# A decoder layer on one core: smaller ScalarE units, resident output weights, keys summed earlier, and a new order of all queues

## What is computed

```python
x = layernorm(x + mamba_and_mlp(x))      # block 1
x = layernorm(x + cross_attention(x, ctx, ctx))  # block 2
x = layernorm(x + lora_experts(x))       # block 3

# block 1
h = x + mamba(rmsnorm(x, w_n1))
#   u, z = split(xn @ in_proj.T); u = silu(causal_conv4(u) + b)
#   dt_r, B, C = split(u @ x_proj.T); dt = softplus(dt_r @ dt_proj.T + b)
#   state[t] = exp(dt[t] * A) * state[t-1] + dt[t] * B[t] * u[t]   (16 states a channel)
#   y = sum over states of state * C + u * D;  out = (y * silu(z)) @ out_proj.T
return h + (silu(hn @ w1.T) * (hn @ w2.T)) @ w3.T      # hn = rmsnorm(h, w_n2)

# block 2: 16 heads, 64 keys. The temperature of the second softmax is a small MLP of three
# means per head over the whole sequence of 1024 queries: mean score, mean of the row maxima,
# mean variance of the first softmax's probabilities
t = exp(clip(mlp(mean_sim, max_sim, entropy_proxy)))
out = softmax(qk / (2 t)) @ V @ Wo.T

# block 3: 8 experts, top 2 by a gate, rank 16, beside a dense matmul
```

## Time and profile before

| what | value |
|---|---|
| median of 3 runs | 3610.53 us (3606.46 to 3612.91) |
| the profiled execution | 3614.06 us, span 3612.0 us, clock of TensorE 0.921 on average |
| TensorE busy | 3056.7 us (85%) |
| VectorE busy | 2799.0 us (77%) |
| ScalarE busy | 2137.4 us (59%) |
| GpSimd busy | 2535.8 us (70%) |
| DMA | 558.49 MB, 47.4% of 16 engines' time |

### The profile page before, as it was taken

One profiled execution on the slowest core, in us unless ns is written; L12 is line 12 of the kernel. 1 busy time (PEld: TensorE's weight loads), 2 busy tenths in 40 slices (PEclk: granted clock), 3 DMA queues, 4 the chain that ended last, 5 costly groups with the idle time before them and its releaser, 6 DMA issues.

```text
span 3612.0 us, 33154 instructions
## 1 busy us (share of the span) xinstructions
PE 3056.7 (85%) x8248; PEld 1460.9 (40%) x8248; DVE 2799.0 (77%) x3376; ACT 2137.4 (59%) x4824; POOL 2535.8 (70%) x1132
## 2 busy tenths in 40 slices
PE   6877677877988987899989868998994898999868
PEld 3433333333434433444434334444442444444444
DVE  3778888888898888888899888888898898822253
ACT  4666666565558457766774586666547857441132
POOL 0557877779998897778889978787798888810000
PEclk9988888889998999999989979999996999999989
DMA  4455555556654564454655634545453444522100
GB/s 174 145 171 201 188 187 199 186 188 221 221 186 147 174 210 132 129 164 147 195 154 184 204 111 146 166 149 177 160 190 110 162 159 162 168 76 76 41 1 24
DMA packets 247160, 558.49 MB, mean 155 GB/s; under 512 B 34748, under 2 KB 35132, under 8 KB 246716
## 3 DMA queue, kind: packets, MB, share of 16 engines
q1 hardware_dynamic: 246972, 556.38, 47.4%
HBM read 515.91 MB, written 40.37 MB: 154 GB/s over the span
## 4 chain that ended last, share of the span: by engine, by line
PE 38%; DVE 10%; ACT 9%; issue 4%; POOL 2%; DMA 0%; DVEq 0%; ACTq 0%; POOLq 0%; SPq 0%
PE ps L1781 22%; PE ps L1878 8%; DVE hb L1558 3%; PE ps L1839 3%; ACT ps L1428 2%; ACT xw L1467 2%; DVE ps L1568 1%; PE ps L1949 1%; PE ps L1914 1%; ACT ps L1252 1%; POOL hb L1194 1%; DVE mxs L1640 1%; PE ps L1982 1%; POOL hb L1204 1%; PE ps L1941 1%
## 5 line engine op out<-in xcount | busy, mean ns | idle before, releaser
L1204 POOL TENSOR_TENSOR hb<-hb,bc 128x1024 f32<-128x1024 f32 x512 | 1205.5, 2355 | 390.4 <-ACT state L1322 225.3
L1194 POOL TENSOR_TENSOR hb<-dtu,bc 128x1024 f32<-128x1024 f32 x512 | 1206.3, 2356 | 161.1 <-DVE ps L1568 153.2
L1781 PE MATMUL ps<-fT,wden 128*128 128x512 f32 x2304 | 1044.4, 608 | 78.9 <-DVE se L1653 25.7
L1252 ACT ACTIVATE ps<-dt,a_neg 128x512 f32<-128x512 f32 x1024 | 689.2, 690 | 588.0 <-DVE hb L1558 586.5
L1781 PEld LDWEIGHTS ps<-fT,wden 128*128 128x128 f32 x2304 | 442.6, 195 | 632.6 <-issue 611.1
L1558 DVE TENSOR_TENSOR_SCAN hb<-ps,state,hb 128x512 f32<-128x512 f32 x512 | 627.6, 1268 | 73.0 <-POOL hb L1194 38.8
L1558 DVE TENSOR_TENSOR_SCAN hb<-ps,hb 128x512 f32<-128x512 f32 x512 | 596.8, 1207 | 88.4 <-POOL hb L1194 63.8
L1568 DVE TENSOR_TENSOR ps<-ps,hb 128x1024 f32<-128x1024 f32 x512 | 624.6, 1220 | 11.6 <-POOL hb L1204 10.9
L1781 PE MATMUL ps<-xnT,wmix 128*128 128x512 f32 x1024 | 492.7, 642 | 81.6 <-DMA wmix<-in_w_mix 44.1
L1878 PE MATMUL ps<-wden,hm 128*128 128x512 f32 x1024 | 466.2, 608 | 34.2 <-DVE res L1611 14.8
L1781 PEld LDWEIGHTS ps<-xnT,wmix 128*128 128x128 f32 x1024 | 208.5, 207 | 361.9 <-issue 305.4
(11 more groups left out here) (248 smaller groups left out, 3535.1 us busy)
## 6 DMA issues: line engine op xcount, KB each, us to landing
bc<-p_dram SPq DMA_DIRECT2D x1024, 256.0 KB, 3.4
wden<-in_w SPq DMA_DIRECT2D x192, 512.0 KB, 4.0
wmix<-in_w_mix SPq DMA_DIRECT2D x128, 512.0 KB, 3.9
z_dram<-ring SPq DMA_DIRECT2D x64, 256.0 KB, 4.5
u<-z_dram SPq DMA_DIRECT2D x32, 512.0 KB, 5.0
watt<-in_w_qof SPq DMA_DIRECT2D x26, 512.0 KB, 4.5
u_dram<-res SPq DMA_DIRECT2D x24, 512.0 KB, 3.4
u<-u_dram SPq DMA_DIRECT2D x24, 512.0 KB, 5.2
```

The lines of the kernel that those rows point to most:

```text
L1194: TTn(hb[:, n % HB], dtu[:, :, :], bc[:, 0, n % BC].unsqueeze(1).broadcast_to([P, 2, CH]), ALU.mult).then_inc(s.s1_ready, 1)
L1204: TTn(hb[:, n % HB], hb[:, n % HB], bc[:, 1, n % BC].unsqueeze(1).broadcast_to([P, 2, CH]), ALU.mult).then_inc(s.s3_done, 1)
L1252: A_(dst, dt[:, p % 2, jj], ACT.Exp, scale=a_neg[:, j, n:n + 1]).then_inc(full_of(key), 1)
L1781: ins = M(dst, a, b, start=start and n == 0, stop=stop and n == len(pairs) - 1)
```

## The change

Seven edits, in the words of the code:

1. `norm`, `xs` and `hs` become four units each, one for each tile. `out` of a chunk writes its Squares to the lower half of `xnT` for every chunk, and `hs` too.
2. `sp1` is cut in two: `sp0` (Abs, Exp) and `sp1` (the two Identities).
3. The four weight tiles of `ou` are loaded once (`load_o`), when the last `z` is done, to the two slots of `wmix` and the upper half of `xnT`. The 64 loads go.
4. `kmean` sums the keys and multiplies them with the summed queries. It stands in stream `s` behind the scores of the first tile. `mean` keeps the two reductions over maxima and variances.
5. `WORK` and `PHASE` are replaced.
6. `LOOK` is replaced.
7. The costs in `parts` follow the new units.

```diff
-    got = [("norm", c), ("xs", c)] + [("tin", c, n) for n in range(KC)]
+    got = [("norm", c, t) for t in range(TT)] + [("xs", c, t) for t in range(TT)] + [("tin", c, n) for n in range(KC)]
...
-        got += [("rms", c), ("hs", c)] + [("to", c, n) for n in range(KC)]
+        got += [("rms", c)] + [("hs", c, t) for t in range(TT)] + [("to", c, n) for n in range(KC)]
...
-    return [("dt", c, j), ("sp1", c, j), ("sp2", c, j), ("sp3", c, j), ("sp4", c, j)]
+    return [("dt", c, j), ("sp0", c, j), ("sp1", c, j), ("sp2", c, j), ("sp3", c, j), ("sp4", c, j)]
...
+            if t == 0 and c % 2:
+                got.append(("kmean", c))
...
     if kind == "norm":
-        part(ACT_, 5.2, ("x_load", c), ("z", c - 2, JB - 1))
-        part(DVE, 0.2, mine())
+        part(ACT_, 0.85 if i < last else 2.6, ("x_load", c), ("z", c - 2, JB - 1))
+        if i == last:
+            part(DVE, 0.2, mine())
     elif kind == "xs":
-        part(ACT_, 3.2, ("norm", c))
+        part(ACT_, 0.8, ("norm", c, last))
...
-        part(PE, 4 * MM, ("gate", c, PAIRS - 1), ("res_load", c), ("f_load", F_FIRST.get(u)),
+        part(PE, 4 * MM, ("gate", c, PAIRS - 1), ("res_load", c), ("o_load", 0),
...
+    elif kind == "sp0":
+        before_c, before_p = pair_of(c * PAIRS + i // 2 - 1)
+        part(ACT_, 1.3, ("dt", *key), ("sp4", c, i - 1) if i % 2 else ("sp4", before_c, 2 * before_p + 1), ("yp", before_c, before_p))
     elif kind == "sp1":
...
-        part(ACT_, 2.68, ("dt", *key), ("sp4", c, i - 1) if i % 2 else ("sp4", before_c, 2 * before_p + 1), ("yp", before_c, before_p))
+        part(ACT_, 1.45, ("sp0", *key))
...
+    elif kind == "kmean":
+        part(DVE, 2.6, ("kv", b))
     elif kind == "mean":
-        part(DVE, 4.0, ("ent", c))
+        part(DVE, 1.0, ("ent", c))
...
-WORK = {"x": 849.2, "w": 145.7, "s": 1219.5, "y": 59.6, "f": 162.7}
+WORK = {"x": 1925.7, "w": 118.4, "s": 1411.9, "y": 1558.6, "f": 210.1}
...
-    "f": (2.25, 28.227, 8.121, 13.061, 16.33, 4.66, 5.08, 6.078),
...
+    "f": (1.383, 20.274, 10.618, 15.423, -9.517, 4.439, 5.932, 6.466),
...
-        elif kind == "ou":
-            first[u] = len(src)
-            src.append(W_O + u[3])
-            release.append((u, u))
...
-LOOK = {"m": 0.319, "l": 0.0, "x": 0.0, "w": 0.043, "s": 0.009, "y": 0.096, "f": 0.0}
+LOOK = {"m": 0.09, "l": 0.037, "x": 0.018, "w": 0.023, "s": 0.043, "y": 0.047, "f": 0.041}
...
+    at(DONE[("z", CHUNKS - 1, JB - 1)], 1, "o_load", 0)
...
+        w_o = [wmix[:, 0], wmix[:, 1]] + [xnT[:, 1, 2 * m:2 * m + 2].rearrange("p c l -> p (c l)") for m in range(2)]
...
+            def load_o():
+
+                filled(sp, ("z", CHUNKS - 1, JB - 1))
+                for q in range(PAIRS):
+                    sp.dma_start(w_o[q], A["w_mix"][W_O + q]).then_inc(s.wo_in, 16)
...
                     ch.link(A_(sp_e, src, ACT.Abs))
-                    ch.link(A_(sp_e, sp_e, ACT.Exp, scale=-1.0))
+                    A_(sp_e, sp_e, ACT.Exp, scale=-1.0).then_inc(s.e_ready, 1)
+                elif kind == "sp1":
+                    act.wait_ge(s.e_ready, c * JB + i + 1)
...
-                elif kind == "mean":
+                elif kind == "kmean":
                     dve.wait_ge(kv_in[b % 2], 64 * (b // 2 + 1))
-                    dve.wait_ge(s.ent_done, c + 1)
-                    dve.wait_ge(s.mx_ready, 2 * TT * (c + 1))
...
-                    wo = f_in(pe, F_FIRST[unit]).rearrange("p (j d) -> p j d", j=2)
+                    if c == 0 and i == 0 and q == 0:
+                        pe.wait_ge(s.wo_in, 16 * PAIRS)
+                    wo = w_o[q].rearrange("p (j d) -> p j d", j=2)
```

More of the change, by code:

```diff
@@ L203, in parts @@
     if kind == "norm":
-        part(ACT_, 5.2, ("x_load", c), ("z", c - 2, JB - 1))
-        part(DVE, 0.2, mine())
+        part(ACT_, 0.85 if i < last else 2.6, ("x_load", c), ("z", c - 2, JB - 1))
+        if i == last:
+            part(DVE, 0.2, mine())
     elif kind == "xs":
-        part(ACT_, 3.2, ("norm", c))
+        part(ACT_, 0.8, ("norm", c, last))
     elif kind == "tin":
-        part(PE, 0.65, ("xs", c), takes=(("xt", c, i),))
+        part(PE, 0.65, ("xs", c, last), takes=(("xt", c, i),))
         part(ACT_, EV, mine(), gives=(("xt", c, i),))
@@ L254, in parts @@
     elif kind == "hs":
-        part(ACT_, 3.2, ("rms", c), ("to", c - 1, KC - 1))
+        part(ACT_, 0.8, ("rms", c), ("to", c - 1, KC - 1))
     elif kind == "to":
-        part(PE, 0.65, ("hs", c), ("query", c - 1, KC - 1), takes=(("ft", c, i),))
+        part(PE, 0.65, ("hs", c, last), ("query", c - 1, KC - 1), takes=(("ft", c, i),))
         part(ACT_, EV, mine(), gives=(("ft", c, i),))
@@ L464, in loaded_after @@
             got[("f_load", n)] = F_RELEASE[n - FSLOTS][1]
+    got[("o_load", 0)] = ("z", CHUNKS - 1, JB - 1)
     for u in RING_USE:
@@ L1131, in _ @@
                     load_z(c, i)
+                elif kind == "o_load":
+                    load_o()
                 elif kind == "u_store":
@@ L1295, in _ @@
                     A_(dst, filled(act, key), ACT.Identity, bias=one_row).then_inc(free_of(key), 1)
-                elif kind == "sp1":
+                elif kind == "sp0":
                     src = filled(act, ("dt", c, i))
@@ L1335, in _ @@
                     if i == 0:
-                        filled(act, ("z", CHUNKS - 1, JB - 1))
-                    A_(xnT[:, half, i], ht[:, i], ACT.Square, accum_out=smo[:, 0, i:i + 1]).then_inc(s.ss2_ready, 1)
+                        filled(act, ("ft", c - 1, KC - 1) if c else ("z", CHUNKS - 1, JB - 1))
+                    A_(xnT[:, 0, i], ht[:, i], ACT.Square, accum_out=smo[:, 0, i:i + 1]).then_inc(s.ss2_ready, 1)
                 elif kind == "rms":
@@ L1341, in _ @@
                 elif kind == "hs":
-                    act.wait_ge(s.rstd2_ready, c + 1)
-                    for t in range(TT):
-                        ins = A_(xnT[:, half, t], ht[:, t], ACT.Copy, scale=smo[:, 2, t:t + 1])
-                    ins.then_inc(s.hs_ready, 1)
+                    if i == 0:
+                        act.wait_ge(s.rstd2_ready, c + 1)
+                    ins = A_(xnT[:, 0, i], ht[:, i], ACT.Copy, scale=smo[:, 2, i:i + 1])
+                    if i == TT - 1:
+                        ins.then_inc(s.hs_ready, 1)
                 elif kind == "to":
@@ L1675, in _ @@
                         rows = slice(32 * q, 32 * q + 32)
-                        ins = V.tensor_copy(sta[rows, 0].rearrange("p (c q) -> p c q", q=4)[:, :, q], ks[rows, 0, :])
-                    ins.then_inc(s.sta_ready, 1)
+                        V.tensor_copy(sta[rows, 0].rearrange("p (c q) -> p c q", q=4)[:, :, q], ks[rows, 0, :])
+                elif kind == "mean":
+                    dve.wait_ge(s.ent_done, c + 1)
+                    dve.wait_ge(s.mx_ready, 2 * TT * (c + 1))
+                    V.tensor_reduce(sta[:, 1, :], mxs[:, :, :].rearrange("p t h -> p h t"), AX, ALU.add)
+                    V.tensor_reduce(sta[:, 2, :], ents[:, :, :].rearrange("p t h -> p h t"), AX, ALU.add).then_inc(s.sta_ready, 1)
                 elif kind == "clip":
@@ L1848, in _ @@
                     for t in range(TT):
-                        ins = turn(dst[:, t * P:(t + 1) * P], xnT[:, half, t, i * P:(i + 1) * P], ident[:, :])
+                        ins = turn(dst[:, t * P:(t + 1) * P], xnT[:, 0, t, i * P:(i + 1) * P], ident[:, :])
                     ins.then_inc(full_of(key), 1)
```

41 lines of the change are left out of this document (18 added, 23 removed), and 8 rows, old and new, of the table PHASE.

## The result

The changed kernel takes 3624.08 us in the median (3615.82 to 3631.79), the kernel before, run beside it, 3608.93 us (3606.37 to 3615.86). The ratio is 1.0035, with a 95% interval of 1.0022 to 1.0048: some 13 us slower, where 27 us less was forecast. The time is inside the range of 3525 to 3650 and on the other side of "no change". The profiled execution took 3622.63 us, span 3620.8 us; that of before had a span of 3612.0 us.

A forecast was written before the change was run, and what follows sets the result against it. No engine is full: the mixer's short queue waits until 2795, TensorE's backlog to 3415, then about 197 us of dependence set the time. 3614.06 - 4 - 23 = 3587 us profiled, 3583.5 by the median; range 3525 to 3650.

The forecast's parts named there:

- no change: Whole kernel: rival that cuts let no mixer unit in and the order only moves waits; 3603 to 3618, chance 0.13.
- The new order, -23: Mixer's chunks: smaller mixer handicap speeds the slow chunks 3 and 6; somewhat less than half of 55 us gained, -23.
- The bounds of -55 to +32: New order's limits: chunks 3 and 6 both fall to 364 us (-55), or a 364 becomes a 396 (+32).
- TensorE's backlog: Behind the mixer's end: rival that delayed dense units leave TensorE more work; 3640 or 3670, over 3618, chance 0.31.
- Resident weights, -4: Output projections, above all chunk 6 behind 2795: 64 loads become 4, less TensorE waiting; -4 us, from -11.5 to 0.
- The cover that I named: TensorE's idle time in 2709 to 2799 hides the new 3.9 to 15.6 us weight wait; 0, up to +15 without.
- Key sums, 0: Scores and mean: chunk 7 moves 2.2 us from mean to scores; chunks 1, 3, 5 hidden by ScalarE; 0.
- Pieces of `norm`, `xs`, `hs`, `sp0` and `sp1`, 0: ScalarE's queue: mixer never gets between ready pieces; 0 (-9 to +3), and 0 for the cut softplus (-16 to +5).
- Tables, 0: ScalarE's table loads: cuts add no further load; a new order may add or save some at 1.28 us each.
- the two signs that I had named: Prediction wrong if mixer's end to chunk 7's scores exceeds 250 us, or mixer's chunks spread as before with another mean.

The follow-up runs named there:

- e1: Kernel before with only the changed kernel's WORK, PHASE and LOOK, its own units kept: 3654.84 us, ratio 1.0118.
- e6: Changed kernel with only the mixer's LOOK set back from 0.09 to 0.319: 3709.38 us, ratio 1.0273.
- e3: Kernel before, its order kept, with only the output weights made resident: 3622.30 us, ratio 1.0026.
- e9: Kernel before, order kept, output weights resident in chunks 0 to 5 (first tile loaded early), streamed in chunks 6 and 7: 3606.16 us, ratio 0.9988.
- e15: Kernel before, order kept, weights resident in chunks 0 to 5 only (first tile early), key sums moved in chunk 7 alone: 3605.86 us, ratio 0.9985.
- e7: Kernel before, order kept, output weights resident, first tile loaded two z units earlier, one wait for each tile: 3617.72 us, ratio 1.0010.
- e14: Changed kernel, order kept, with all key sums back in the mean and weights still resident: 3625.94 us, ratio 1.0039.
- e11: Changed kernel, order and pieces kept, with output weights streamed and key sums in the mean again: 3632.55 us, ratio 1.0056.
- e4: Kernel before, its order kept, with only the key sums moved behind the scores of tile 0: 3621.39 us, ratio 1.0029.
- e5: Kernel before, its order kept, with resident output weights and moved key sums, without the pieces: 3628.19 us, ratio 1.0046.

## Why the prediction was wrong, by its own steps

**The new order, -23, is the step that failed most.** I put its gain where chunks 3 and 6 were slower than chunk 4, and that part came: 27 us. The step left out that the sum over the eight chunks is what counts, and gave the other six chunks no share: they lost 31. It also put nothing behind the mixer, where the new order left 4 us of work and cost 5 us of waiting and clock. The reason was wrong too. I argued that a smaller handicap lets the mixer win against dense units; e1 has that handicap with the old units and the mixer ends 31 us later. e6, the handicap alone, goes the way that I argued, but by stalls in two chunks. The ranks are compared between streams whose every unit moved, and nothing can be read from one number. The bounds of -55 to +32 held: without the edits the order is worth +20, with both -4. The two are not to be added up one by one: against the forecast of -27 the measured +13 is 40 us off, and counted with the edits first, 21 of them are the edits' (-4 forecast, +17 measured) and 19 the order's; counted with the order first, it is the order's 43, and the edits are 3 us better than forecast.

**TensorE's backlog** was named as the rival on the other side, with the right place and the right sign. Its size was 4.2 us of work, against the 26 that I gave it, and the mixer's end did not move at all; its chance was 0.31. The other 5 us behind the mixer, 1.4 of a wait and 3.6 of a lower clock, are in no term and no rival; without them the loss would be some 8 us of the 13, by the traces.

**Resident weights, -4.** The 4.3 us of waits did go, and the wait in their place was 8.7 us, inside 3.9 to 15.6. The cover that I named did not show: the mixer of e3 is 7 to 9 us late from 843 to 2458. It is 2.5 us late from 2511 on, but e9 and e15, which were not late, gain the same 6.7 us there, with the clock. What the step left out is what waits next. At the very place where I looked for the gain, right behind 2795, the removed waits of 1.36 us had been waits in the shade of VectorE. At the order before the edit is +9, and e7, without the new wait, still loses 6.5 us behind 2830 in its trace (+4 by its ratio, with an interval from 0). In the changed order the term has its forecast sign: -6 (e14 against e11).

**Key sums, 0.** Chunk 7 is right to 0.1 us. Chunks 1, 3 and 5 are wrong: "ScalarE is the slower of the two and hides it" holds for the scores' own chain, not for the mixer's scans that stand behind them in VectorE's queue. The term is +10 at the order before. The sums took 3.7, 4.0 and 4.8 us in these chunks, not 2.2, as I had taken the duration from a place where GpSimd is idle. Of that 2.2 us are seen to reach the end, from chunk 5; most of the rest goes with a lower clock around 2265 to 2308, and its cause stays open.

**Pieces of `norm`, `xs`, `hs`, `sp0` and `sp1`, 0.** The queue of the changed kernel has no mixer unit between two pieces, as worked out; the softplus does go between them, as this line-up of ScalarE shows (L1279 is `xs`, L1314 is the first half of `sp0`, L1318 begins `sp1`):

```profile
325.15 1.32 ACT L1279 ACTIVATE stage<-stage,smi 128x512 f32<-128x512 f32 x2
327.37 0.60 ACT L1314 ACTIVATE spt<-ps 128x512 f32<-128x512 f32 x1 [0.90 <-PE ps L1843]
...
328.54 0.71 ACT L1279 ACTIVATE stage<-stage,smi 128x512 f32<-128x512 f32 x1
329.15 0.71 ACT L1318 ACTIVATE spt<-spt,ones_t 128x512 f32<-128x512 f32 x1
```

I had expected four in a row; they are not. What the cuts are worth by themselves no run tells: at the order before they change nothing, and the changed order was drawn with them.

**Tables, 0.** The page counts 4821 instructions of ScalarE against 4824. At 1.28 us a load this is nothing either way.

Of the two signs that I had named for a wrong prediction the first came: from the mixer's end to the scores of chunk 7 it is 266 us, over the 250 given, and 9 us over the 257 of before with the same cut, so that the bound itself was too low. The second came otherwise: the chunks spread less than before, at nearly the same mean (383.2 against 382.7 us).

## What to carry to other kernels

When an edit comes with a new order of the queues, time the edit at the old order and the old work at the new one before believing either; here the same edit was worth +9 in one and -6 in the other. A gap in one queue counts only as far as the next thing that the queue waits for is there: look one wait further, and at the clock behind it. Lay two traces of one order step by step before naming a cause: a step that comes late where nothing was changed is to be looked up in the clock. Work moved on an engine that several streams share has to be priced against what stands behind it in the queue, at every place to which it moves, with durations from that place.

## What the runs showed of the hardware

A VectorE product of two operands with 4 elements a row took 1.90 us at 2088.87 in e4, while GpSimd ran its product, and 0.15 us at 3437.05 in the changed kernel with GpSimd idle. The reduction beside it, which reads one operand, took 1.21 us at both places. Under two products of GpSimd's in a row it took 2.71 us (2762.51 in e4). So a tiny instruction can be priced only where its neighbour's work is known.

Taking away 1.36 us of TensorE's waits in one place was followed by a granted clock of 0.67 where it had been 1.00, and by 16 matmul instructions of 9.92 us instead of 7.11 (9.85 and 8.68 in e3 and e5). The kernel that waits a little more there, e9, had the clock at 1.00. A faster start of a stage was followed by a slower clock in it.

The same instructions, started within 0.2 us of the same time, ran at different granted clocks in two traces: 8 matmul instructions took 5.40 us in e4 and 3.70 us before, from 2264.6 in both. And such differences came back from kernel to kernel: the 32 instructions of chunk 6's queries took 15.67 us in all six traces of the changed order and its redraw and 13.97 us in all eight of the old order.
